# First norm's statistics on ScalarE, and new places for scatters, staged parts, softmax and Wo's pieces in the attention step

## What is computed

```python
mod = (_silu(L0_c) @ L0_wmod).reshape(8, 6, 1, -1)      # sa, ca, ga, sb, cb, gb
h = _layernorm(x) * (1 + ca) + sa
xn = _layernorm(h, ln_gamma, ln_beta)
k, v, r = (einsum('btc,dc->btd', xn, W) for W in (Wk, Wv, Wr))
kv = k * v
csum = cumsum(kv * pow(td, t_idx), axis=1)
wkv = tf * kv + td * shifted(csum)
x = x + ga * einsum('btc,dc->btd', sigmoid(r) * wkv, Wo)
h = _layernorm(x) * (1 + cb) + sb
x = x + gb * (moe(h, group 0) + moe(h, group 1)) / 2    # each: 32 experts, top 2, SwiGLU 512 -> 256 -> 512
```

## Time and profile before

| | |
|---|---|
| median of 3 runs | 5015.96 us (5013.2 to 5016.27) |
| profiled execution | 5032.62 us, its span 5030.9 us |
| PE | 4643.5 us busy, 92% of the span |
| DVE | 3011.9 us, 60% |
| ACT | 1635.8 us, 33% |
| POOL | 2804.4 us, 56% |
| mean granted TensorE clock | 0.951 |
| HBM | 235 GB/s over the span |

### The profile page before, as it was taken

The page is one execution under the profiler, slowest core; times in us unless marked ns, Lnnn a source line. Parts: engine busy times, 40 slices in busy tenths (PEclk is TensorE's granted clock), DMA queues, the critical chain, the costliest instruction groups (busy, mean ns, idle before and its releaser), DMA issues.

```text
span 5030.9 us, 89180 instructions
## 1 busy us (share of the span) xinstructions
PE 4643.5 (92%) x22649; PEld 3825.1 (76%) x22649; DVE 3011.9 (60%) x6077; ACT 1635.8 (33%) x4093; POOL 2804.4 (56%) x2303
## 2 busy tenths in 40 slices
PE   6999999989988999499989998999999999999998
PEld 4777777777777777377777776888788888888886
DVE  5888888888888888444444443554344444444443
ACT  2344444444444444122222222332222222222222
POOL 2576666666666666544454544555455555555554
PEclk8999999999999999799999999999999999999999
DMA  6666565656665656589999989999999989998897
GB/s 234 214 198 212 181 199 181 207 185 213 186 208 185 207 183 199 204 248 277 274 276 268 272 265 271 266 278 248 282 237 245 236 230 253 241 240 215 220 230 192
DMA packets 434624, 1152.46 MB, mean 229 GB/s; under 512 B 59361, under 2 KB 59362, under 8 KB 415666
## 3 DMA queue, kind: packets, MB, share of 16 engines
q0 software_dynamic: 182512, 454.27, 38.8%
q1 hardware_dynamic: 231106, 619.79, 36.2%
q10 hardware_dynamic: 20736, 75.51, 4.0%
HBM read 719.35 MB, written 463.57 MB: 235 GB/s over the span
## 4 chain that ended last, share of the span: by engine, by line
PE 39%; DMA 13%; issue 4%; POOL 2%; DVE 1%; POOLq 0%; SPq 0%; DVEq 0%; ACT 0%
DMA out<-c_yo,c_idx 12%; PE ps L1322 11%; PE ps L1324 11%; PE ps L1323 11%; PE ps L1331 4%; PE ps L1350 2%; DMA c_wt<-wsp_d 1%; POOL out L1313 1%; POOL c_xg L1280 1%; POOLq L1305 0%; DVE c_yo L1577 0%; POOL list_d L1285 0%; DMA list_d<-pairs,sidx 0%; DMA c_lists<-list_d,c_rowu 0%; DVE c_xl L1565 0%
## 5 line engine op out<-in xcount | busy, mean ns | idle before, releaser
L1313 POOL DMA_INDIRECT out<-c_yo,c_idx x576 | 919.0, 1595 | 922.0 <-DMA out<-c_yo,c_idx 481.4
L1322 PE MATMUL ps<-c_wt,c_xh 128*128 128x512 f32 x2304 | 964.7, 419 | 27.6 <-issue 20.3
L1324 PE MATMUL ps<-c_wt,c_xl 128*128 128x512 f32 x2304 | 911.0, 395 | 0.0
L1323 PE MATMUL ps<-c_wt,c_xh 128*128 128x512 f32 x2304 | 904.9, 393 | 0.0
L1280 POOL DMA_INDIRECT c_xg<-h2g_d,c_idx x576 | 566.9, 984 | 512.2 <-DVE c_yo L1577 406.8
L1561 DVE TENSOR_TENSOR c_hh<-ps,c_sil 128x256 f32<-128x256 f32 x576 | 244.1, 424 | 926.1 <-ACT c_sil L1404 926.0
L1577 DVE SCALAR_TENSOR_TENSOR c_yo<-ps,c_wc,c_xg 128x512 f32<-128x512 f32 x576 | 432.4, 751 | 521.2 <-PE ps L1324 265.9
L444 PE MATMUL ps<-xTh,wTh 128*128 128x512 f32 x1536 | 640.1, 417 | 46.9 <-DVE cs L841 34.8
L1409 ACT CAST c_xh<-ps 128x512 fp32r<-128x512 f32 x576 | 337.1, 585 | 957.5 <-PE ps L1331 956.1
L445 PE MATMUL ps<-xTl,wTh 128*128 128x512 f32 x1536 | 627.0, 408 | 0.0
L446 PE MATMUL ps<-xTh,wTl 128*128 128x512 f32 x1536 | 625.4, 407 | 0.0
(11 more groups left out here) (202 smaller groups left out, 7767.7 us busy)
## 6 DMA issues: line engine op xcount, KB each, us to landing
c_wt<-wsp_d SPq DMA_DIRECT2D x69, 2048.0 KB, 11.4
sraw<-wex SPq DMA_DIRECT2D x290, 256.0 KB, 3.5
wsp_d<-shigh SPq DMA_DIRECT2D x288, 256.0 KB
wsp_d<-sraw SPq DMA_DIRECT2D x288, 256.0 KB
c_wt<-wsp_d SPq DMA_DIRECT2D x69, 1024.0 KB, 12.5
xin<-x SPq DMA_DIRECT2D x34, 1024.0 KB, 7.9
h2g_d<-mod_d SPq DMA_DIRECT2D x128, 256.0 KB, 6.2
out<-xin SPq DMA_DIRECT2D x32, 1024.0 KB, 6.7
```

The source lines that it names most:

```text
L1313: nc.gpsimd.indirect_dma_start(out=out, out_offset=bass.IndirectOffsetOnAxis(ap=idx[:, n:n + 1], axis=0), in_=yo[:, n % 4, :], in_offset=N ...
L1322: nc.tensor.matmul(o, lh, rh, start=first, stop=False)
L1323: nc.tensor.matmul(o, lh, rl, start=False, stop=False)
L1324: return nc.tensor.matmul(o, ll, rh, start=False, stop=last)
```

## The change

- `DVE_LOW`, the jobs of a step whose low half VectorE makes, goes from 4, 5, 6 to 1, 5, 8. VectorE's and GpSimd's places for the low halves follow.
- Wo's pieces are jobs 5 to 8 of a row instead of 2 to 5. GpSimd multiplies pieces 5 and 6 before the step's scatters and 7 and 8 behind the first eight.
- The first norm's statistics leave VectorE (`norm_front` part 0, but for the first two steps). ScalarE sums x with Identity and its accumulator, scales the sums to -mean, sums squares of x - mean, and makes variance plus epsilon; the unused full output goes to the tile `hit`. Part 1 on VectorE adds -mean.
- VectorE runs `topk` first in the step, not behind chunk 0.
- GpSimd keeps 16 scatters a step; six instead of five are in the step after. The low halves of jobs 6 and 7 stand before `receive` 1.
- ScalarE's order changes: the high half of a step's first job moves to the step before, `soften` goes ahead of `chunk_r` 0, `hi` 0 behind jobs 2 and 3, job 8 and `chunk_k` 3 before `turned`.

```diff
@@ -79,14 +79,14 @@
 
 JOBS = 40
 PER_STEP = 10
-DVE_LOW = (4, 5, 6)
-WO_PART = {2: 0, 3: 1, 4: 2, 5: 3}
+DVE_LOW = (1, 5, 8)
+WO_PART = {5: 0, 6: 1, 7: 2, 8: 3}
 SPLITS = JOBS - len(WO_PART)
 
 
 def split_no(j):
 
-    return j if j < 2 else j - len(WO_PART)
+    return j if j < 5 else j - len(WO_PART)
 
 
 def jn(b, j, per, k):
...
@@ -350,7 +352,7 @@
 
             def stage_out(b, j):
 
-                wait(sp, low_of(j), lows(b, j))
+                gate(sp, (low_of(j), lows(b, j)))
                 if j not in WO_PART:
                     _, _, rows, part = split_at(b, j)
                     for col, tile in zip(PARTS[part], (shigh[:, j % 2].bitcast(F32), sraw[:, j % 4])):
@@ -492,8 +494,8 @@
 
                 pe.wait_ge(s_split, cnt(b, s - 1, 4, 4))
                 if s == 1:
-                    pe.wait_ge(low_of(3), lows(b, 3))
-                    pe.wait_ge(low_of(5), lows(b, 5))
+                    pe.wait_ge(low_of(7), lows(b, 7))
+                    pe.wait_ge(low_of(8), lows(b, 8))
                 for j in range(TJ):
                     t = slice(j * P, (j + 1) * P)
                     bank_free(pe, b, s, OUTP + j)
@@ -615,40 +617,88 @@
                     wait(act, proj_done, cnt(b, s, 12, 12))
                     nc.scalar.copy(xTh[:, k, :], bank(s, FRONTT + k)).then_inc(x_hi, 1)
 
+            def sums(b, s, js):
+
+                u = (s + 2) % 4
+                junk = hit[:].rearrange("p k r e -> p (k r e)")
+                if js[0] == 0:
+                    n = (s + 2) // 4 + 1
+                    act.wait_ge(x_in[u], 16 * (b + n) if isinstance(b, int) else b * 16 + n * 16)
+                    wait(act, f_mean, cnt(b, s - 1, 1, 1))
+                    wait(act, at_sum, cnt(b, s - 2, 1, 1))
+                    if isinstance(b, int) and b == 0 and s == 0:
+                        act.wait_ge(zeroed, 96)
+                for j in js:
+                    wait(act, f_sq, cnt(b, s - 1, 4, 4))
+                    wait(act, f_sum, cnt(b, s, 4, j))
+                    nc.scalar.activation(junk, xin[:, u, j, :], ACT.Identity,
+                                         accum_out=fsum[:, j:j + 1]).then_inc(f_sum, 1)
+
+            def mean(b, s):
+
+                act.wait_ge(f_sum, cnt(b, s, 4, 4))
+                wait(act, f_sq, cnt(b, s - 1, 4, 4))
+                wait(act, h_half, cnt(b, s + 1, 4, 4))
+                nc.scalar.activation(fnm[:], fsum[:], ACT.Copy, scale=-1.0 / C).then_inc(f_mean, 1)
+
+            def squares(b, s, js):
+
+                u = (s + 2) % 4
+                junk = hit[:].rearrange("p k r e -> p (k r e)")
+                for j in js:
+                    act.wait_ge(f_mean, cnt(b, s, 1, 1))
+                    wait(act, f_var, cnt(b, s + 1, 1, 1))
+                    wait(act, f_sq, cnt(b, s, 4, j))
+                    nc.scalar.activation(junk, xin[:, u, j, :], ACT.Square, bias=fnm[:, j:j + 1],
+                                         accum_out=fsq[:, j:j + 1]).then_inc(f_sq, 1)
+                if js[-1] == TJ - 1:
+                    act.wait_ge(f_sq, cnt(b, s, 4, 4))
+                    wait(act, f_rstd, cnt(b, s + 1, 1, 1))
+                    nc.scalar.activation(vaf[:], fsq[:], ACT.Identity, bias=epsc[:], scale=1.0 / C).then_inc(f_var, 1)
+
             def step(b, s, first):
                 back_too = not (first and s == 0)
                 at = s * PER_STEP
-                stage_hi(b, at)
+                if first and s == 0:
+                    stage_hi(b, 0)
                 stage_hi(b, at + 1)
                 chunk_k(b, s, 0)
-                chunk_r(b, s, 0)
-                hi(b, s, 0)
                 if not (first and s < 2):
                     soften(b, s - 2)
+                chunk_r(b, s, 0)
                 stage_hi(b, at + 2)
                 stage_hi(b, at + 3)
+                hi(b, s, 0)
                 stage_hi(b, at + 4)
                 normed(b, s)
                 stage_hi(b, at + 5)
+                sums(b, s, (0, 1))
                 chunk_k(b, s, 1)
+                sums(b, s, (2, 3))
+                mean(b, s)
+                chunk_r(b, s, 1)
                 stage_hi(b, at + 6)
-                chunk_r(b, s, 1)
                 chunk_k(b, s, 2)
+                squares(b, s, (0, 1))
+                stage_hi(b, at + 7)
+                squares(b, s, (2, 3))
+                chunk_r(b, s, 2)
                 hi(b, s, 1)
+                stage_hi(b, at + 8)
+                chunk_k(b, s, 3)
                 if back_too:
                     turned(b, s)
-                chunk_r(b, s, 2)
-                chunk_k(b, s, 3)
                 hi(b, s, 2)
-                stage_hi(b, at + 7)
-                stage_hi(b, at + 8)
-                front(b, s, (0, 1))
+                stage_hi(b, at + 9)
                 chunk_r(b, s, 3)
-                front(b, s, (2, 3))
+                front(b, s, range(KC))
                 hi(b, s, 3)
+                if s < 3:
+                    stage_hi(b, at + 10)
+                else:
+                    stage_hi(b + 1, 0)
                 if back_too:
                     logits(b, s)
-                stage_hi(b, at + 9)
 
             normed(0, -1)
             front(0, -1, range(KC))
@@ -691,9 +741,6 @@
                 else:
                     dst, high = sraw[:, j % 4].bitcast(F32R), shigh[:, j % 2]
                 nc.gpsimd.tensor_tensor(dst, sraw[:, j % 4], high.bitcast(F32), ALU.subtract).then_inc(low_pool, 1)
-                for i in (j + 1,) if j < 3 else (j + 1, j + 2):
-                    if i in WO_PART:
-                        scale_wo(b, i)
 
             def lo(b, s, dc):
                 pool.wait_ge(s_hi, cnt(b, s, 4, dc + 1))
@@ -714,40 +761,44 @@
 
             def step(b, s, first):
                 old = not (first and s < 2)
+                older = not (first and s < 3)
                 at = s * PER_STEP
+                if older:
+                    scatter(b, s - 3, 10, 13)
+                rstd(f_var, vaf, h_ready, rsf, f_rstd, b, s + 1)
                 stage_lo(b, at)
-                if not (first and s < 3):
-                    scatter(b, s - 3, 11, 13)
-                rstd(f_var, vaf, h_ready, rsf, f_rstd, b, s + 1)
-                stage_lo(b, at + 1)
+                if older:
+                    scatter(b, s - 3, 13, 16)
                 receive(b, s, 0)
-                if not (first and s < 3):
-                    scatter(b, s - 3, 13, 14)
-                lo(b, s, 0)
-                if not (first and s < 3):
-                    scatter(b, s - 3, 14, 16)
                 stage_lo(b, at + 2)
                 rstd(g_var, vag, z_ready, rsg, g_rstd, b, s + 1)
                 stage_lo(b, at + 3)
+                lo(b, s, 0)
+                stage_lo(b, at + 4)
                 if not (first and s == 0):
                     rstd(b_var, vab, h2_ready, rsb, b_rstd, b, s - 1)
+                if s == 0:
+                    scale_wo(b, 5)
+                    scale_wo(b, 6)
                 if old:
                     scatter(b, s - 2, 0, 8)
+                if s == 0:
+                    scale_wo(b, 7)
+                stage_lo(b, at + 6)
+                if s == 0:
+                    scale_wo(b, 8)
+                stage_lo(b, at + 7)
                 receive(b, s, 1)
                 if old:
                     scatter(b, s - 2, 8, 9)
                 lo(b, s, 1)
                 receive(b, s, 2)
-                stage_lo(b, at + 7)
-                lo(b, s, 2)
-                stage_lo(b, at + 8)
                 if old:
                     scatter(b, s - 2, 9, 10)
+                lo(b, s, 2)
                 receive(b, s, 3)
-                if old:
-                    scatter(b, s - 2, 10, 11)
+                stage_lo(b, at + 9)
                 lo(b, s, 3)
-                stage_lo(b, at + 9)
 
             rstd(f_var, vaf, h_ready, rsf, f_rstd, 0, 0)
             rstd(g_var, vag, z_ready, rsg, g_rstd, 0, 0)
...
@@ -789,9 +840,12 @@
                         row = b + s // 4
                         dve.wait_ge(modf_in, 16 * (row + 1) if isinstance(b, int) else b * 16 + (s // 4 + 1) * 16)
                     wait(dve, frontT_done, cnt(b, s - 1, 4, 4))
+                    early = isinstance(b, int) and 4 * b + s < 2
+                    wait(dve, f_mean, cnt(b, s - 2, 1, 1))
                     for j in range(TJ):
-                        V.scalar_tensor_tensor(out=hb[:, j, :], in0=xin[:, u, j, :], scalar=mvf[:, j, 0:1],
-                                               in1=mod[:, CA1, :], op0=ALU.subtract, op1=ALU.mult).then_inc(h_half, 1)
+                        V.scalar_tensor_tensor(out=hb[:, j, :], in0=xin[:, u, j, :],
+                                               scalar=mvf[:, j, 0:1] if early else fnm[:, j:j + 1], in1=mod[:, CA1, :],
+                                               op0=ALU.subtract if early else ALU.add, op1=ALU.mult).then_inc(h_half, 1)
                 elif part == 2:
```

(18 more changed lines are left out.)

## The result

The kernel after takes 5067.33 us (median of 7 runs, 5062.44 to 5083.43) against 5018.47 for the kernel before on the same chip (7 runs, 5013.2 to 5043.67): a ratio of 1.0087, with a 95% interval of 1.0064 to 1.011. The profiled execution took 5063.42 us, its span 5061.7; before they were 5032.62 and 5030.9.

The account below looks back on a forecast made before the run. VectorE's queue, with a DMA wait inside, was taken to bound the attention steps through chunk 1's scan. Mean step 58.1 against 61.2 us gave 87 + 7 us less 1, together 93: 4923 us, 8 in 10 for 4810 to 5012.

Parts of the forecast that it names:

- Chunk 1: VectorE's queue in a step: chunk 1 was to start at 37.0 us instead of 41.3.
- the turns with GpSimd: VectorE and GpSimd alternate on SBUF: norm part 1 ends at 9.3, part 2 takes 2.6 us more.
- Rival A: VectorE and GpSimd take no turns and the clock stays up: mean step 55.5 us, 4844 us; chance 0.17.
- Second chain: GpSimd's `receive` 1 from 45.2 leads to ScalarE's k of chunk 3, ready at 48.8; step ends at 56.6.
- The sign named for "wrong": On ScalarE: the forecast is wrong if the high half of part 7 or 8 waits over 4 us.
- part 1 comes in behind chunk 0, part 8 behind chunk 2: VectorE's low halves: before chunk 1 two of 0.6 us go, one comes, and a 3.17 us wait goes.
- the end of the step: TensorE after chunk 3's scan at 51.7: `front` goes on, and 1.4 + 3.5 us later the step ends at 56.6.
- s=3: The step with the loop's jump: forecast at 59 us, against 57 for s=1 and 2.
- paid back in turns: VectorE's earlier `topk` and the missing wait for GpSimd gain nothing, lost again to SBUF turns with GpSimd.
- That taking the statistics off VectorE gains nothing by itself: First norm's statistics, 2.9 us on VectorE, count as nothing on the path: VectorE would only wait longer for the projection.
- Rival C: Slower: ScalarE's k of chunk 3 hangs on part 6's landing at 53; mean step 62.6 us, 5059 us; chance 0.16.
- rival B: Part 5's writes take 8.5 us as today, delaying part 7's high half: mean step 60.4 us, 4991 us; chance 0.17.

Follow-up runs that it names:

- the second experiment: The changed kernel with GpSimd's `receive` 1 ahead of the low halves of parts 6 and 7: 5039.91 us, ratio 1.0007 against the kernel before.
- The first experiment: The changed kernel with VectorE's low half of part 8 behind chunk 3 instead of ahead of it: 5007.82 us, ratio 0.9947 against the kernel before.
- the kernel with three moves: The changed kernel with part 8's low half behind chunk 3, `receive` 1 first, ScalarE's k 3 ahead of parts 7 and 8: 4872.39 us, 0.9669 against before.

## Why the prediction was wrong

**Bound of before: right.** The scan of chunk 1 was what TensorE waited for, and the change took that wait away.

**Chunk 1: the wait gone as forecast, the place early.** Forecast 37.0, measured 34.8 in the median. `topk`, part 1 and chunk 0 end at 12.2 in step 25 (12.9), and part 2 of the norm takes 4.82 for four (5.3). So the turns with GpSimd took place, but not all where they were put: part 1 was to be stretched and took 2.73 in every one of the 23 steps, while `topk` took 5.2 in step 25 instead of 3.7. nmg and `place` took 2.7 us, not 3.7. Rival A had chunk 1 at 34.4, which is where it came, though not for A's reason; A's time, 4844, fell with the wait in `front` and its clock. The wait of 2 to 4 us in projection 3, named as a sign, did not come, as chunk 2's scan ended at 41.1 in step 25, when v of chunk 3 wanted its bank (41.2).

**Second chain: right up to k 3.** High half of part 7 at 43.8 in step 25 (43), `receive` 1 at 45.8 (45.2), k of chunk 3 ready at 48.8 (48.8). No table load stands at the squares. The terms inside were off in both directions, so that 48.8 is in part luck: the scatters ended at 40.6, not 42.3, and the write took 7.8 us from its first half's issue, not 5, but it was issued earlier, at 36.0. The sign named for "wrong" did show: part 7 waited over 4 us.

**The step that failed: "part 1 comes in behind chunk 0, part 8 behind chunk 2".** It is the second of these low halves. It was costed at nothing, because the statistics "make room for part 8". But room isn't what counts: the low half waits for a high half that ScalarE makes just ahead of k 3, so it can't use the room, and comes when chunk 3 would. A low half counted as 0.6 in the prediction, which is what one takes where VectorE works alone; at 48 GpSimd goes from one two-input operation into the next, and it takes 3.0. Chunk 3 starts 2.4 us late. Nearly all of that is the stretch: the high half is ready at 48.2, and a low half of 0.68 from there would end at 48.9, 0.1 behind k 3; the second experiment, where it takes 1.4, has chunk 3 at 49.0. The rows were there: 6.13 us for part 1 of the norm in the earlier trace rows, and the claim about turns was applied to the norm and not to this line. With the line moved, the ratio fell by 1.4%. The Trainium skill, SBUF — State Buffer, section "SBUF: two separate sides", has the lock as one for a whole instruction; the trace agrees: both start at 1663.97, GpSimd's goes first, its next one (1665.19 to 1666.46) too, and VectorE's ends 0.55 later, at 1667.01.

**A term mis-sized: the end of the step.** "1.4 + 3.5 later the step ends" was 4.9 us; step 25 took 6.99 from `front`'s second part on. Before, the clock was low in projection 3, since `back` waited ahead of it, and the logits came at full clock. A row of TensorE before, the end of step 17:

```profile
1156.33 3.68 PE L476 MATMUL ps<-rws,h2T 128*128 128x64 f32 x32
```

A wait moved to `front` moves the lower level on to the logits: 5.33 us in the mean, from their first to their last. The forecast let the stall go from one place to another and left its clock behind. That is 2.1 us, and the wait was 6.36 us long instead of "up to 2": with k at 48.8 as forecast, projection 3 ended at 47.1, while the forecast had it end between 49.0 and 51.6. The first experiment shows this term by itself: with chunk 3 at 48.8, as forecast, steps with s=1 and 2 take 58.9 us in the mean, not 57.

**Another: s=3.** Forecast 59, measured 65.4, where s=1 and 2 have 61.4. The jump costs 4.0 us now, 1.8 before (62.6 against 60.8). Part of it is the clock: the logits took 6.93 us. The step from 23 to 24, on TensorE, and the clock there:

```profile
1543.10 2.82 PE L489 MATMUL ps<-ident,hb 128*128 128x128 f32 x12 [6.68 <-DVE cs L895]
1545.72 6.93 PE L478 MATMUL ps<-rws,h2T 128*128 128x64 f32 x32
1554.59 0.79 PE L446 MATMUL ps<-xTh,wTh 128*128 128x512 f32 x1 [1.94 <-issue]
```
```profile
1546.00:1549.00 3.00, 3.00 (x16) 3.00 (x16) 1.11 (x2) 1.58 (x3) 2.13 (x3) 0.50 0.52 104
```

In the kernel with three moves s=3 takes 55.8. Why the level stays low through all the logits in some steps and not in others was not tested.

**That the move of `topk` is "paid back in turns": wrong.** With the softmax it gains 1.1%. **"That taking the statistics off VectorE gains nothing by itself": right for this change**, and only because VectorE waited anyway; with that gone they are worth 2.1%.

**Sum.** The mean was forecast at 58.1 and is 62.5: 2.4 for chunk 3, 2.1 for the end of the step, more in s=3, less in s=0. 4.4 times 31 is 136, and 4923 + 136 = 5059, beside 5067 measured. **Rival C** had 5059 too, by another way: k of chunk 3 was to hang on the landing of part 6. It did not: the high half of part 8 (1663.34) has no wait. The DMA wait was on part 5's write, as in rival B, and took 7.8 us as B counts (from the first half's issue), short of B's 8.5. Right number, wrong mechanism.

## What to carry to other kernels

When a stall is taken away, lay out the next one with everything that stood around the old: its queue, the clock behind it, and who else reads SBUF then. Don't cost a moved step by the room that it gets but by when its input comes; a step without a deadline goes behind the one with a deadline, not into the gap ahead of it. Where one result hangs on three engines' orders, two of them mended alone show 0.8 and 1.4%, and all three together 4.1%: test them together before one is given up.

## What the runs showed of the hardware

- The subtraction of 128x512 on VectorE took 0.68 us alone. Ahead of chunk 3 in after, beside GpSimd's 1.27 us operations, it took 3.01 to 3.06 us in all 23 steps; with another order on GpSimd 1.4 us in the median, and behind the scan 3.7.
- A write of 256 KB halves landed 6.5 us after its second half's issue behind the 1 MB store of h2 and a 256 KB copy, and 3.2 us with the store behind it and the copy 6 us ahead.
- In a wait of TensorE the granted clock was 1.00 for its first 3.8 us and 0.54 over its last 2.5 (step 25); the lower level then held for 4.5 us of transposes and logits.
- 32 logits matmuls took 3.68 us at full clock and 6.93 at 0.50. The lower level was there for 9.8 us of a step before, 10.5 after, and 2.8 with three moves.
- ScalarE's squares with accumulator took 0.72 and 0.19 us for the read. They ran between two sigmoids without a table load of 1.28 us; a step has two such loads, one at the softmax and one at the next sigmoid.
